# P times V of an attention block as plain float32 matmuls, two heads at a time, in place of high and low fp32r halves

## The reference, cut to what matters

```python
x = x + 0.5 * ffn(layernorm(x))
# attention, 16 heads of 64, causal, with a linear distance bias per head
q, k, v = split(layernorm(x) @ w_qkv)            # [16, 512, 1024] each
sim  = (q * 64**-0.5) @ k.T - slope[h] * |i - j|  # masked where j > i
attn = softmax(sim)
out  = attn @ v                                   # the product that is changed
x = x + out @ w_out + b_out
x = x + 0.5 * ffn(layernorm(x))
# ffn(h) = gelu(h @ w1 + b1) @ w2 + b2, hidden 1024
```

## Time and profile before

| | us |
|---|---|
| three runs | 2590.16, 2591.95, 2593.57 (median 2591.95) |
| the profiled execution, whole | 2591.63 |
| its span, first to last instruction | 2589.8 |
| mean granted TensorE clock | 0.995 of full |
| VectorE and ScalarE busy, share of the span | 78%, 63% |
| GpSimd busy, share | 27% |
| DMA engines, mean bandwidth | 88 GB/s |

### The profile page before, as it was taken

The page is one execution under the profiler, slowest core; times in us unless marked ns, Lnnn a source line. Parts: engine busy times, 40 slices in busy tenths (PEclk is TensorE's granted clock), DMA queues, the critical chain, the costliest instruction groups (busy, mean ns, idle before and its releaser), DMA issues.

```text
span 2589.8 us, 46603 instructions
## 1 busy us (share of the span) xinstructions
PE 2481.1 (96%) x16256; PEld 2248.2 (87%) x16256; DVE 2029.6 (78%) x5222; ACT 1622.8 (63%) x3672; POOL 705.9 (27%) x1130
## 2 busy tenths in 40 slices
PE   6999999999999999999999999999999999999997
PEld 5888889888898888888888888888888889888896
DVE  6877969779697786968869687796877969779684
ACT  4856838467384764837658385583856838467383
POOL 1322313223232222313224132231322313223231
PEclk9999999999999999999999999999999999999998
DMA  4615326063360623506244161441715326063260
GB/s 136 153 25 125 88 49 151 14 139 74 70 143 1 153 60 90 123 18 146 50 105 108 25 157 32 115 98 30 159 25 127 86 53 150 11 139 74 68 136 9
DMA packets 103817, 227.71 MB, mean 88 GB/s; under 512 B 18080, under 2 KB 36768, under 8 KB 103584
## 3 DMA queue, kind: packets, MB, share of 16 engines
q1 hardware_dynamic: 103584, 224.73, 38.1%
HBM read 14.95 MB, written 8.39 MB: 9 GB/s over the span
## 4 chain that ended last, share of the span: by engine, by line
PE 79%; DVE 12%; DMA 3%; ACT 3%; issue 2%; POOL 1%; SPq 0%; DVEq 0%; ACTq 0%
PE psA L324 23%; PE psC L324 20%; PE psD L324 16%; PE psB L324 10%; PE psB L456 9%; DMA stack<-qk 3%; DVE gl L713 3%; DVE ptl L713 2%; DVE P L794 1%; DVE xn L743 1%; DVE xtl L713 1%; PE psB L349 1%; DVE gh L772 1%; ACT gt L597 1%; DVE ol L713 1%
## 5 line engine op out<-in xcount | busy, mean ns | idle before, releaser
L974 POOL TENSOR_SCALAR P<-P,rs 128x512 f32<-128x512 f32 (+3 forms) x1024 | 534.0, 534 | 1195.8 <-DVE rs L784 1195.8
L611 ACT ACTIVATE P<-P,mx 128x512 f32<-128x512 f32 (+3 forms) x1024 | 570.0, 558 | 252.1 <-DVE mx L794 252.1
L794 DVE CUSTOM_DVE_ANT_0 P<-psA,dist 128x512 f32<-128x512 f32 (+3 forms) x1024 | 440.3, 486 | 42.1 <-PE psA L324 40.3
L713 DVE TENSOR_TENSOR ptl<-psB,pth 128x512 fp32r<-128x512 f32 (+1 forms) x512 | 410.3, 816 | 30.0 <-ACT pth L652 27.7
L324 PE MATMUL psA<-stack 128*128 128x512 f32 (+3 forms) x2048 | 380.7, 328 | 28.3 <-DMA stack<-qk 28.2
L324 PEld LDWEIGHTS psA<-stack 128*128 128x128 f32 x2048 | 321.4, 190 | 57.5 <-DMA stack<-qk 34.4
L456 PE MATMUL psB<-ident,P 128*128 128x128 f32 x2560 | 328.9, 276 | 23.2 <-POOL P L974 22.3
L652 ACT ACTIVATE pth<-psB 128x512 fp32r<-128x512 f32 (+1 forms) x512 | 342.5, 702 | 4.5 <-PE psB L456 1.4
L456 PEld LDWEIGHTS psB<-ident,P 128*128 128x128 f32 x2560 | 285.0, 141 | 54.6 <-POOL P L974 33.5
L597 ACT ACTIVATE gt<-psA,b1c 128x512 f32<-128x512 f32 x256 | 174.4, 688 | 186.1 <-PE psA L324 184.2
L713 DVE TENSOR_TENSOR gl<-gt,gh 128x512 fp32r<-128x512 f32 x256 | 208.5, 814 | 8.8
(11 more groups left out here) (120 smaller groups left out, 6280.1 us busy)
## 6 DMA issues: line engine op xcount, KB each, us to landing
stack<-qk SPq DMA_DIRECT2D x512, 256.0 KB, 3.6
stack<-qk SPq DMA_DIRECT2D x512, 128.0 KB, 3.5
x<-in_L_attn_x SPq DMA_DIRECT2D x16, 512.0 KB, 4.3
out_y<-x SPq DMA_DIRECT2D x16, 512.0 KB, 3.9
raw<-in_L_ffn_w SPq DMA_DIRECT2D x2, 512.0 KB, 5.6
raw<-in_L_ffn_w SPq DMA_DIRECT2D x1, 1024.0 KB, 9.0
rawq<-in_L_attn_w_qkv SPq DMA_DIRECT2D x1, 1024.0 KB, 7.7
rawk<-in_L_attn_w_qkv SPq DMA_DIRECT2D x1, 1024.0 KB, 9.8
```

The lines of the kernel that those rows point to most:

```text
L611: e.activation(p, p, ACT.Exp, bias=mx[:, r, i:i + 1], scale=-1.0, accum_out=sm[:, r, i:i + 1]).then_inc(s_ex.sem, 1)
L713: return e.tensor_tensor(dst, src, hi.bitcast(F32), ALU.subtract)
L794: e.tensor_tensor_reduce(out=P[h % 2][:, cs], in0=psA[:, cs], in1=dist[:, T - w:T], scale=-SLOPE[h], scalar=BIG, op0=ALU.add, op1=ALU.min, ...
L974: e.tensor_scalar(p, p, rs[:, s % 4, i:i + 1], 1.0, ALU.mult, ALU.mult).then_inc(s_nz.sem, 1)
```

## The change

`values` now takes a pair of heads. For each of the four blocks j it issues one plain float32 matmul for the first head of the pair and one for the second; the first writes partitions 0 to 63 of the output bank (64 weight columns), the second partitions 64 to 127. V is kept as one float32 tile (`v_copy` on ScalarE; VectorE has no part in it), and the transposed P as one float32 tile per head in four buffers `PT`: ScalarE copies its first 512 columns (`turned_first`), VectorE the other 768 (`turned_rest`). The output of a pair is copied once by ScalarE (`out_copy`, 128x512); the addition of halves is gone. `values` of pair c runs in the odd step 2c+3 alone; even steps, and the step s = 16, have none.

```diff
-        values = [("values", s - 2)] if 0 <= s - 2 < H else []
+        values = [("values", s // 2 - 1)] if s >= 3 and s % 2 else []
...
-            def values(b, h):
+            def values(b, c):
...
-                    mm(pv[:, 128 * j:T], lhs, pth[h % 2][:, ks], j == 0, False)
-                    last = mm(pv[:, 128 * j:T], lhs, ptl[h % 2][:, ks], False, j == NT - 1)
+                    for i in range(2):
+                        h = 2 * c + i
+                        if j == 0:
+                            e.wait_ge(s_c0.sem, s_c0.at((b, h)))
+                        if j == 1:
+                            e.wait_ge(s_c1.sem, s_c1.at((b, h)))
+                        last = mm(pv[64 * i:64 * i + 64, 128 * j:T], vv[:, j, h % 4, :], PT[h % 4][:, ks],
+                                  j == 0, j == NT - 1)
...
-                    if s >= 2:
-                        values(b, s - 2)
+                    if s >= 3 and s % 2:
+                        values(b, s // 2 - 1)
...
+            def v_copy(b, tile):
+                _, g, u = tile
+                e.wait_ge(s_pj.sem, s_pj.at((b, tile)))
...
+                e.activation(v[g % 2][:, 2 * u:2 * u + 2, :, :],
+                             bk(bank_of(tile)).rearrange("p (t h d) -> p t h d", t=2, h=4),
+                             ACT.Copy).then_inc(s_vc.sem, 1)
...
-                e.activation(pth[h % 2][:, ps], psB[:, ps], ACT.Copy).then_inc(s_hp.sem, 1)
+            def turned_first(b, h):
+                e.wait_ge(s_tp.sem, s_tp.at((b, h, 0)))
+                if h >= 4:
+                    e.wait_ge(s_pv.sem, s_pv.at((b, h // 2 - 2)))
+                e.activation(PT[h % 4][:, 0:T], psB[:, 0:T], ACT.Copy).then_inc(s_c0.sem, 1)
+
+            def out_copy(b, c):
+                e.wait_ge(s_pv.sem, s_pv.at((b, c)))
+                e.activation(o[:, c, :], bk(bank_of(("values", c))), ACT.Copy).then_inc(s_oa.sem, 1)
...
-                residue(ptl[h % 2][:, ps], psB[:, ps], pth[h % 2][:, ps]).then_inc(s_lo.sem, 1)
-
-            def add_halves(b, h):
+            def turned_rest(b, h):
+                e.wait_ge(s_tp.sem, s_tp.at((b, h, 1)))
+                if h >= 4:
+                    e.wait_ge(s_pv.sem, s_pv.at((b, h // 2 - 2)))
+                e.tensor_copy(PT[h % 4][:, T:PW], psB[:, T:PW]).then_inc(s_c1.sem, 1)
```

More of the change, by code:

```diff
@@ L20, in build @@
     PW = 1280
-    PARTS = (slice(0, 512), slice(512, PW))
     at = [16512]
@@ L65, in build @@
     stack = [place(f"stack{i}", [128, 3, T], F32R, R + 8192 + 6144 * i) for i in range(2)]
-    v = [place(f"v{i}", [128, NT, 4, 128], F32R, R + 20480 + 8192 * i) for i in range(2)]
+    v = [place(f"v{i}", [128, NT, 4, DH], F32, R + 20480 + 8192 * i) for i in range(2)]
     P = [place(f"P{i}", [128, PW], F32, R + 36864 + 4 * PW * i) for i in range(2)]
-    pth = [place(f"pth{i}", [128, PW], F32R, R + 47104 + 8 * PW * i) for i in range(2)]
-    ptl = [place(f"ptl{i}", [128, PW], F32R, R + 47104 + 4 * PW + 8 * PW * i) for i in range(2)]
+    PT = [place(f"pt{i}", [128, PW], F32, R + 47104 + 4 * PW * i) for i in range(4)]
     g_at = {1: [0, 4096, 8192, 12288, 22528, 47104, 51200, 55296],
@@ L152, in build @@
     proj = [(b, t) for b in B for t in tiles]
+    proj_qk = [(b, t) for b, t in proj if t[0] != "v"]
+    proj_v = [(b, t) for b, t in proj if t[0] == "v"]
+    pairs = [(b, c) for b in B for c in range(NC)]
     class Signal:
@@ L165, in build @@
     s_tp = Signal("tp_done", per_part)
-    s_pv = Signal("pv_done", heads)
+    s_pv = Signal("pv_done", pairs)
     s_pj = Signal("pj_done", proj)
@@ L173, in build @@
     s_ex = Signal("ex_done", per_block)
-    s_hp = Signal("hp_done", per_part)
-    s_oc = Signal("oc_done", heads)
-    s_ph = Signal("ph_done", proj)
+    s_c0 = Signal("turned_first_copied", heads)
+    s_oa = Signal("out_copied", pairs)
+    s_vc = Signal("v_copied", proj_v)
+    s_ph = Signal("ph_done", proj_qk)
     s_lh = Signal("lh_done", units)
@@ L182, in build @@
     s_rc = Signal("rc_done", [(b, h, half) for b, h in heads for half in (1, 0)])
-    s_lo = Signal("lo_done", per_part)
-    s_oa = Signal("oa_done", heads)
-    s_pl = Signal("pl_done", proj)
+    s_c1 = Signal("turned_rest_copied", heads)
+    s_pl = Signal("pl_done", proj_qk)
     s_ll = Signal("ll_done", units)
@@ L227, in ring_free @@
         elif b > 0:
-            e.wait_ge(s_oa.sem, s_oa.at((b - 1, H - 1)))
+            e.wait_ge(s_oa.sem, s_oa.at((b - 1, NC - 1)))
             e.wait_ge(s_ll.sem, s_ll.at((1, b, 1)))
@@ L238, in ring_free @@
                 e.wait_ge(s_ll.sem, s_ll.at((1, pb + 1, before[1])))
+        elif before[0] == "v":
+            e.wait_ge(s_vc.sem, s_vc.at((pb, before)))
         else:
@@ L373, in dn @@
                 elif f == 1 and b > 0:
-                    e.wait_ge(s_lo.sem, s_lo.at((b - 1, H - 1, 1)))
-                    e.wait_ge(s_oa.sem, s_oa.at((b - 1, H - 1)))
+                    e.wait_ge(s_c1.sem, s_c1.at((b - 1, H - 1)))
+                    e.wait_ge(s_oa.sem, s_oa.at((b - 1, NC - 1)))
                 elif f == 2 and b + 1 < NB:
@@ L378, in dn @@
                 elif f == 2:
-                    e.wait_ge(s_lo.sem, s_lo.at((b, H - 1, 1)))
-                    e.wait_ge(s_oa.sem, s_oa.at((b, H - 1)))
+                    e.wait_ge(s_c1.sem, s_c1.at((b, H - 1)))
+                    e.wait_ge(s_oa.sem, s_oa.at((b, NC - 1)))
                 ts = slice(t * 128, t * 128 + 128)
@@ L397, in out_proj @@
                 elif t == 0:
-                    e.wait_ge(s_lo.sem, s_lo.at((b, H - 1, 1)))
+                    e.wait_ge(s_c0.sem, s_c0.at((b, H - 1)))
+                    e.wait_ge(s_c1.sem, s_c1.at((b, H - 1)))
                 e.wait_ge(s_ol.sem, s_ol.at((b, t)))
@@ L450, in transposes @@
                 for j in range(NT):
-                    if n > 0 and j < 2:
-                        e.wait_ge(s_lo.sem, s_lo.at((*heads[n - 1], j)))
+                    if n > 0 and j == 0:
+                        e.wait_ge(s_c0.sem, s_c0.at(heads[n - 1]))
+                    if n > 0 and j == 1:
+                        e.wait_ge(s_c1.sem, s_c1.at(heads[n - 1]))
                     for i in range(j, NT):
@@ L459, in transposes @@
                 last.then_inc(s_tp.sem, 1)
-            def values(b, h):
[L462 to L465, removed]
+            def values(b, c):
+                ring_free(e, b, ("values", c))
+                pv = bk(bank_of(("values", c)))
+                e.wait_ge(s_vc.sem, s_vc.at((b, ("v", c // 2, 1))))
+                vv = v[(c // 2) % 2]
                 for j in range(NT):
@@ L550, in tile_parts @@
         def tile_parts(tile, dst_lo):
[L552 to L556, removed]
             plane = {"q": (0, 3), "k": (1, 2)}[tile[0]][1 if dst_lo else 0]
@@ L563, in proj_hi @@
             def proj_hi(b, tile):
+                if tile[0] == "v":
+                    v_copy(b, tile)
+                    return
                 e.wait_ge(s_pj.sem, s_pj.at((b, tile)))
[L565 to L576, removed]
+                c = tile[1]
+                if (b, c) != (0, 0):
+                    pb, pc = (b, c - 1) if c else (b - 1, NC - 1)
+                    for i, stacked in enumerate(s_sq if tile[0] == "q" else s_sk):
+                        e.wait_ge(stacked.sem, stacked.at((pb, 2 * pc + i, 1)))
                 dst, src = tile_parts(tile, False)
                 e.activation(dst, src, ACT.Copy).then_inc(s_ph.sem, 1)
+            def v_copy(b, tile):
+                _, g, u = tile
+                e.wait_ge(s_pj.sem, s_pj.at((b, tile)))
+                if g >= 2:
+                    e.wait_ge(s_pv.sem, s_pv.at((b, 2 * g - 3)))
+                elif b > 0:
+                    e.wait_ge(s_pv.sem, s_pv.at((b - 1, NC - 1)))
+                e.activation(v[g % 2][:, 2 * u:2 * u + 2, :, :],
+                             bk(bank_of(tile)).rearrange("p (t h d) -> p t h d", t=2, h=4),
+                             ACT.Copy).then_inc(s_vc.sem, 1)
             def ln_hi(L, b, u):
@@ L622, in attention @@
                     first, second = slots(s)
-                    if s >= 3:
-                        half(b, s - 3)
+                    if s >= 4 and s % 2 == 0:
+                        out_copy(b, s // 2 - 2)
                     if more:
@@ L635, in attention @@
                     if 1 <= s <= H:
-                        turned_hi(b, s - 1, 0)
-                        turned_hi(b, s - 1, 1)
+                        turned_first(b, s - 1)
                     if more:
@@ L833, in attention @@
                             biased(b, s, n)
-                    if s >= 3:
-                        add_halves(b, s - 3)
                     if 0 < s < H:
@@ L843, in attention @@
                     if 1 <= s <= H:
-                        turned_lo(b, s - 1, 0)
-                        turned_lo(b, s - 1, 1)
+                        turned_rest(b, s - 1)
                     if more:
```

9 lines of the change are left out of this document (removed).

## The result

The changed kernel takes 2734.69 us (median of 4, 2731.84 to 2739.57) where the kernel before, on the same chip, takes 2591.22: a ratio of 1.0554, 95% interval 1.0535 to 1.0574. The forecast was 2753 us, in a stated range of 2655 to 3000. The profiled execution took 2737.11 us.

What follows compares the result with a forecast made beforehand. The prediction took TensorE, busy 96% of the span, to bound the kernel. From 2591.6 us it added 115 for a new wait and 58 for values, and took off 12 for relief: 2753 us, range 2655 to 3000.

Steps and rivals of the forecast that it cites:

- The stall: Before the transposes, after even steps 2 to 12: TensorE newly waits 1.20 us for GpSimd's scaling, 96 times, +115 us.
- 0.06 us to spare: Kernel before, end of an even step: values and scores cover the chain from q to the transposes by this margin.
- The values term: TensorE's matmuls of values for a pair of heads: 2.88 us against 2.43, +0.45 us, 128 pairs, +58 us.
- Four passes side by side: In values, a float32 matmul makes four passes and the two heads' column groups run together: 2.27 us.
- the lag of 0.45 us: In a pair's values, matmuls start in program order, so the second head starts half a matmul late; bounds 0 and 0.91.
- 2.7 to 3.1: Expected length in us from a pair's first values matmul to the next scores, if the forecast is right.
- The cost of going from one width to the other: Around a pair's values, changing from one kind of matmul to another: 0.08 us, twice, 0.16 us a pair.
- emptied array: Rival: every change between 64 and 128 columns empties the array, 0.56 us more a pair, +72 us, 2825 us; chance 0.09.
- The relief: Less VectorE and ScalarE work shortens waits at output projection and next start: 0.8 us x 15 elements, -12 us.
- The rival of turns taken: In values, the two column groups run one after the other: 4.70 us a pair, 2985 us in all; chance 0.27.
- the one pass: Rival: in values, a plain float32 matmul makes one pass, 1.17 us a pair, -161 us, 2534 us; chance 0.03.
- the missing wait: Rival: the transposes don't wait, as the chain from q closes in time; 2638 us, chance 0.06.

Runs made afterwards that it cites:

- Experiment 1: Changed kernel with the last exponential (ScalarE) and second inverse (VectorE) moved ahead of the second projection tile's evacuation and low half; 2592.79 us, 0.9997 against the kernel before.
- experiment 5: Kernel before, with values of the even heads cut to one matmul of 512 columns in place of eight, output incomplete; 2591.51 us, ratio 0.9996.
- experiment 10: Kernel before, complete, with only the last exponential and second inverse moved ahead of the second projection tile; 2589.26 us, ratio 0.9990.
- experiment 2: Changed kernel with the loops of values exchanged: all four matmuls of the first head, then all four of the second; 2913.59 us.
- experiment 4: Changed kernel with V and the transposed P kept as bfloat16 tiles, so values runs on rounded operands; 2536.30 us.
- experiment 6: Kernel before, even heads' values cut to one matmul, plus last exponential and second inverse ahead of the second projection tile; 2582.47 us, ratio 0.9963.
- experiment 8: Kernel before with the end of the attention rearranged: step 13's v tile in step 14, step 14's exponentials and second inverse early; 2608.11 us, ratio 1.0063.
- experiment 3: Changed kernel with step 13's v tile projected in step 14, and step 14's exponentials, second inverse and normalisation moved early; 2678.69 us.

## Why the prediction was right

**The stall was there, at its size.** Forecast 1.20 us, 96 times, 115 us. Two heads take 12.80 - 11.55 = 1.25 us more than before, of which 0.02 belong to `values` (below): 1.23 us, 118 us. Experiment 1 removes the wait by order alone; experiment 5 makes the same wait in the old kernel by removing its cover. These two show the cause from both sides. The 1.33 us of experiment 1 are more, since its order also gives what it gives to the old kernel (907.22 - 895.73 = 11.49 us for two heads in experiment 10, in place of 11.55). The reading of 0.06 us to spare was wrong (experiment 5): the transposes already waited a little in the kernel before, as the 1.18 for 1.09 in the earlier trace rows hints.

**The values term was mis-sized.** Forecast +0.45 us a pair (+58 us). Four passes side by side was right (experiments 2 and 4). Wrong was the lag of 0.45 us, taken from the belief that matmuls start in program order: both groups start at 961.58, and experiment 2 shows a group overtaking. Matmuls and weight loads of the pair in the timeline, two looks:

```profile
961.58 0.65 PE L326 MATMUL psC<-pt,v 128*64 128x512 f32 x2
```
```profile
961.58 0.20 PEld L326 LDWEIGHTS psC<-pt,v 128*64 128x64 f32 x4
962.07 0.14 PEld L326 LDWEIGHTS psC<-pt,v 128*64 128x64 f32 x2 [0.28 <-issue]
962.49 0.14 PEld L326 LDWEIGHTS psC<-pt,v 128*64 128x64 f32 x2 [0.28 <-issue]
```

The stretch of 2.30 us lies below the 2.7 to 3.1 that the forecast named as its sign. The cost of going from one width to the other was the forecast's 0.16 us: 0.09 at the start (961.58, where the pace of the v tile would give 961.37 + 0.12 = 961.49), and 0.07 on the scores behind, from start to start (963.89 to 965.28, 1.39 for the 1.32 before). So the pair costs 2.30 + 0.16 = 2.46 us against 1.22 + 1.22 = 2.44: +0.02 us, +3 us in all. The 0.56 more of an emptied array did not come. So the rule on draining (TensorEngine Tiling (Array Packing), Key Properties, in the Trainium skill) may hold, but at a price of 0.16 us a pair, not 0.72.

**The relief was worth nothing.** Forecast -12 us. The wait for the low half of o stayed (10.9 and 10.3 us): in both kernels the chain ahead of it is the last gelu and its split, not the addition that I blamed. At the next start the last two tiles ahead of the scores did take 0.39 us less (1071.61 to 1074.36, before 1012.12 to 1015.26), about the 0.3 forecast, but TensorE then ran into the DMA of the stack, whose wait is 38.3 us now, 10 more than before.

**What the sum left out: the clock.** The changed kernel spends 86 us at the lower level, the one before 28: 58 more, 29 us lost. Of the 17 stretches in mid-run, 8 stand in step 15, where TensorE waits 0.34 + 1.41 = 1.75 us (1.23 before), and 9 at the start of an attention. There the wait for the stack's DMA is 1.9 to 2.2 us from the second element on, some 0.5 more than before. In the five kernels that keep the halves (before and experiments 5, 6, 8, 10), 72 of these 75 waits last at most 1.72 us, and the low clock follows none of them; it follows two of the three others, which last 1.94 to 1.97 us. No experiment changes this wait alone, so its part in the loss is likely and not shown.

Sum as measured: 2591.6 + 118 + 3 + 29 = 2742, and the profiled execution took 2737. The forecast was 55 us too high in `values`, and too low by 3 in the wait, 12 in the relief and 29 in the clock. The direction and the larger term come from the right mechanism. That the total lies within 18 us is luck: the misses cancelled.

The rival of turns taken (2985 us) fell with the stretch of 2.30 us, the emptied array (2825) with the 0.16, the one pass (2534) with experiment 4, the missing wait (2638) with the chain.

## What to carry to other kernels

When work moves between steps, ask what it covered: here 1.22 us of matmuls stood between a projection and the transposes that wait for its evacuation, and the engine that was 96% busy lost them as soon as they left. Before removing work from a busy engine, read how much spare time the other loops have; in the old kernel cutting 127 us from TensorE gained nothing, and taking q out of the chain as well gained only 9 us. A few hundredths of a microsecond between a release and its use are no spare time: compare them with a place where the engine is known to wait. A lighter second engine pays only when the order of work lets TensorE reach it: the float32 form needed two changes of order to be worth 1.1%. And a longer wait can cost twice, once by itself and once by the clock: read the granted clock behind it.

## What was not expected of the hardware

Two matmuls of 64 columns in different column groups start together, and a group starts its matmul ahead of three records of the other group's that come earlier in the program (experiment 2). Two float32 matmuls of 512 columns side by side take 0.91 us together (961.58 to 962.49), the time of four passes of one. What brings the granted clock down is settled only in part. In mid-run it falls, in every kernel here, only in or just behind a wait of TensorE: of 1.41 us in step 15 (2.02 us in experiment 5) or of 1.75 to 2.4 us, most often 1.9 or more, at the start of an attention. Removing the waits of step 15 removed all of the first kind (experiment 3), but the same waits stayed without a fall in experiment 1, and the second kind fell from 9 to 4 in experiment 3, which didn't touch its wait. Why a wait is followed by a fall in one element and not in the next, no run tells.
